# K and Q projections written transposed by the matmul, and plain loads in place of transposing DMAs, in a fused attention and FFN kernel

## The reference, cut to what matters

```python
xn = layernorm(x)                       # x: [4, 4096, 2048]
K = einsum('bse,ae->bsa', xn, Wk)       # a = 2048
Q = einsum('bse,ae->bsa', xn, Wq)
V = einsum('bse,ae->bsa', xn, Wv)
scores = einsum('bqa,bka->bqk', Q, K) / sqrt(2048)      # then the causal mask
attn = round(softmax(scores) @ V, 4 decimals)
ffn  = fake_quant(relu(fake_quant(xn) @ fake_quant(kernel) + fake_quant(bias)))
out  = x + attn + ffn
```

## Time and profile before

| | us |
|---|---|
| median of 2 runs | 5945.97 |
| the two runs | 5921.64 and 5970.3 |
| profiled execution | 5971.41 |
| its span, slowest core (core 4) | 5969.9 |
| spans of the other cores | 5839.6 to 5943.7 |

### The profile page before, as it was taken

How to read it: one execution, slowest core, us unless ns; L and a number is a source line. 1 busy time by engine, 2 the same in 40 slices (tenths; PEclk the granted TensorE clock), 3 DMA queues, 4 the chain that set the end, 5 groups by cost and what they waited for, 6 DMA issues and landing times.

```text
span 5969.9 us, 38440 instructions; the slowest of 8 cores (5839.6 to 5969.9 us)
## 1 busy us (share of the span) xinstructions
PE 3581.1 (60%) x9611; PEld 886.2 (15%) x9801; DVE 1084.3 (18%) x1473; ACT 655.8 (11%) x717; POOL 209.9 (4%) x87
## 2 busy tenths in 40 slices
PE   2877787878787466666206831336364537465776
PEld 0212212121212111111001210001010101111111
DVE  1111101010100322220495630111010101101001
ACT  1101101010100222221211210000000000000000
POOL 1000000000000000000050000000000000000000
PEclk9767867676769565667557965555555555555555
DMA  8011000101001411101321112322323233232422
GB/s 152 36 36 43 36 35 36 36 36 36 36 29 47 94 39 42 38 33 46 106 85 43 56 29 60 85 81 84 79 81 81 86 87 80 89 82 79 129 69 98
DMA packets 501827, 380.75 MB, mean 64 GB/s; under 512 B 429537, under 2 KB 429697, under 8 KB 487297
## 3 DMA queue, kind: packets, MB, share of 16 engines
q1 hardware_dynamic: 445362, 277.56, 16.7%
q10 hardware_dynamic: 49152, 75.51, 3.3%
q0 software_dynamic: 7120, 25.22, 2.6%
HBM read 243.94 MB, written 75.51 MB: 54 GB/s over the span
## 4 chain that ended last, share of the span: by engine, by line
PE 49%; DMA 16%; issue 11%; DVE 7%; SPq 6%; ACT 6%; another core or an unknown queue 4%; ACTq 0%; DVEq 0%; POOLq 0%
PE pspool L445 12%; DMA pool<-qS 10%; PE pspool L467 8%; PE pspool L987 8%; SPq L970 6%; PE pspool L625 5%; DMA pool<-vS 5%; PE pspool L849 4%; PE pspool L1043 4%; PE pspool L427 2%; PE pspool L1079 2%; ACT pool L334 2%; ACT pool L336 2%; PE pspool L364 1%
## 5 line engine op out<-in xcount | busy, mean ns | idle before, releaser
L987 PE MATMUL pspool<-pool 128*128 128x512 bf16 x1127 | 649.1, 585 | 858.9 <-DMA pool<-kS 667.1
L445 PE MATMUL pspool<-pool 128*128 128x512 bf16 x2001 | 871.5, 517 | 209.5 <-remote 40.7
L625 PE MATMUL pspool<-pool 128*128 128x512 bf16 x996 | 467.6, 545 | 133.0 <-ACT pool L632 42.9
L467 PE MATMUL pspool<-pool 128*128 128x512 bf16 x2005 | 494.4, 408 | 4.0 <-PE pspool L427 0.9
L849 PE MATMUL pspool<-pool 128*128 128x512 bf16 x1003 | 272.6, 392 | 223.8 <-remote 182.9
L1043 PE MATMUL pspool<-pool 128*128 128x512 bf16 x559 | 296.0, 599 | 135.5 <-DMA pool<-vS 81.4
L987 PEld LDWEIGHTS pspool<-pool 128*128 128x128 bf16 x1152 | 121.9, 106 | 1388.1 <-issue 1386.2
L1079 PE MATMUL pspool<-pool 128*128 128x512 bf16 x567 | 232.1, 554 | 111.1 <-DMA pool<-vS 107.3
L427 PE MATMUL pspool<-pool 128*128 128x128 bf16 x512 | 135.1, 268 | 248.7 <-DVE pool L351 191.4
L445 PEld LDWEIGHTS pspool<-pool 128*128 128x128 bf16 x2048 | 145.2, 102 | 903.1 <-issue 899.5
L467 PEld LDWEIGHTS pspool<-pool 128*128 128x128 bf16 x2048 | 210.4, 103 | 275.4 <-issue 71.7
(11 more groups left out here) (118 smaller groups left out, 1932.9 us busy)
## 6 DMA issues: line engine op xcount, KB each, us to landing
pool<-vS SPq DMA_DIRECT2D x288, 256.0 KB, 2.7
pool<-emb SPq DMA_DIRECT2D x32, 1024.0 KB, 5.9
pool<-x_own SPq DMA_DIRECT2D x32, 1024.0 KB, 5.5
pool<-fker SPq DMA_DIRECT2D x32, 1024.0 KB, 5.0
kS<-pool ACTq DMA_DIRECT2D x32, 512.0 KB, 2.6
vS<-pool ACTq DMA_DIRECT2D x32, 512.0 KB, 2.6
out<-pool ACTq DMA_DIRECT2D x16, 1024.0 KB, 4.0
pool<-kS SPq DMA_TRANSPOSE x576, 2.7
```

What stands on the lines that cost most here:

```text
L445: e.matmul(psB[:, fo:fo + fw], xnT[:, 512 * c + 128 * t:512 * c + 128 * t + 128], W1[:, E * c + fo:E * c + fo + fw], start=st, stop=sp),
L467: e.matmul(pv, xnT[:, 512 * c + 128 * t:512 * c + 128 * t + 128], W2[:, E * c + fo:E * c + fo + fw], start=st, stop=sp),
L625: e.matmul(psB[:, fo:fo + fw], xnT2[:, 512 * c + 128 * t:512 * c + 128 * t + 128], WQ[:, E * c + fo:E * c + fo + fw], start=st, stop=sp),
L987: st=(c == 0), sp=(c == NCH - 1): e.matmul(pa, qt[par][T][:, 128 * c:128 * c + 128], ktb[ks][:, 512 * c:512 * (c + 1)], start=st, stop=sp),
```

## The change

K and Q are computed already transposed. The weights become the stationary operand (128x128 blocks of `W1` or `WQ`) and the normalised strip `xnT` the moving one, so each result is 128 values of `a` by 512 rows. For each strip and each of the 16 blocks `ca` of `a`, 16 matmuls accumulate into one 512-column bank of `psB`, which is now split into four buffers `bK[0..3]` used in turn. ACT evicts each bank (128x512) into one of two small buffers and stores it. `kS` and `qS` are laid out as [16, 128, rows], so the attention stage loads its tiles with plain DMAs.

The number of matmuls, their size (128x512) and the number of weight loads stay as they were. The order around them changes: in stage 1 a strip is now V for all four tiles, then all of K, then the 16 transpose batches of the next strip in one piece; `pend` is gone. In stage 2 the layer norms of the next strip are recorded ahead of the strip's Q matmuls, and its 32 batches after them.

```diff
-    kS = nc.dram_tensor("kS", [S, E], BF16, kind="Internal").ap()
+    kS = nc.dram_tensor("kS", [NCH, 128, S], BF16, kind="Internal").ap()
-    qS = nc.dram_tensor("qS", [OWNT * 128, E], BF16, kind="Internal").ap()
+    qS = nc.dram_tensor("qS", [NCH, 128, OWNT * 128], BF16, kind="Internal").ap()
...
+        bK = [Buf(f"psK{r}") for r in range(4)]
...
-                for c in range(NCH):
-                    for fi, (fo, fw) in enumerate(_splits(E)):
-                        p.step("PE", lambda e, c=c, t=t, fo=fo, fw=fw,
-                               st=(c == 0), sp=(c == NCH - 1):
-                               e.matmul(psB[:, fo:fo + fw],
-                                        xnT[:, 512 * c + 128 * t:512 * c + 128 * t + 128],
-                                        W1[:, E * c + fo:E * c + fo + fw], start=st, stop=sp),
-                               reads=[b_xnTc[t], b_W1], writes=[bB[(2 * fo) // E]])
-                    if c % 4 == 3 and pend:
-                        fn = pend.pop(0)
-                        fn()
-                p.step("ACT", lambda e: e.activation(kev, psB[:, 0:E], AF.Copy),
-                       reads=[bB[0], bB[1]], writes=[b_kev])
...
+            xn_reads = [b_xnTc[0], b_xnTc[1], b_xnTc[2], b_xnTc[3], b_W1]
+            for ca in range(NCH):
+                r = ca % 4
+                pk = psB[:, 512 * r:512 * (r + 1)]
+                for ce in range(NCH):
+                    p.step("PE", lambda e, pk=pk, ca=ca, ce=ce,
+                           st=(ce == 0), sp=(ce == NCH - 1):
+                           e.matmul(pk, W1[:, E * ce + 128 * ca:E * ce + 128 * ca + 128],
+                                    xnT[:, 512 * ce:512 * ce + 512], start=st, stop=sp),
+                           reads=xn_reads, writes=[bK[r]])
+                ev = ca % 2
+                p.step("ACT", lambda e, pk=pk, ev=ev: e.activation(kste[ev], pk, AF.Copy),
+                       reads=[bK[r]], writes=[b_kste[ev]])
+                p.dma("ACT", "kev", lambda e, ca=ca, s=s, ev=ev: e.dma_start(
+                    out=kS[ca][:, 512 * s:512 * (s + 1)], in_=kste[ev]),
+                    reads=[b_kste[ev]], writes=[b_ktS])
+            if s + 1 < NSTRIP:
+                for t in range(4):
                     for j in range(NCH // 4):
-                        pend.append(lambda strip=s + 1, t=t, j=j: p1_tbatch(strip, t, j))
+                        p1_tbatch(s + 1, t, j)
...
         for so in range(NSO):
...
+            if so + 1 < NSO:
+                for t in range(4):
                     p2_ln(so + 1, t)
...
+                           e.matmul(pk, WQ[:, E * ce + 128 * ca:E * ce + 128 * ca + 128],
+                                    xnT2[:, 512 * ce:512 * ce + 512], start=st, stop=sp),
+                           reads=xn2_reads, writes=[bK[r]])
...
                         out=qt[par][T][:, 128 * c:128 * c + 128],
-                        in_=qS[128 * slot:128 * (slot + 1), 128 * c:128 * (c + 1)],
-                        transpose=True),
+                        in_=qS[c][:, 128 * slot:128 * (slot + 1)]),
                         reads=[b_qtS], writes=[b_qt[par][T]])
...
                         out=ktb[ks][:, 512 * c:512 * (c + 1)],
-                        in_=kS[512 * s:512 * (s + 1), 128 * c:128 * (c + 1)],
-                        transpose=True),
+                        in_=kS[c][:, 512 * s:512 * (s + 1)]),
                         reads=[b_ktS], writes=[b_ktb[ks]])
```

More of the change, by code:

```diff
@@ L493, in build_nc @@
         o_xnT2 = al.take(NCH * 512 // 2)
-        o_qev = al.take(E // 2)
+        o_qst = al.take(512)
         o_ci2 = al.take(E)
@@ L615, in build_nc @@
                 p2_nxbatch(0, t, j)
-        pend2 = []
         for so in range(NSO):
-            for t in range(4):
-                slot = 4 * so + t
-                for c in range(NCH):
-                    for fi, (fo, fw) in enumerate(_splits(E)):
-                        p.step("PE", lambda e, c=c, t=t, fo=fo, fw=fw,
-                               st=(c == 0), sp=(c == NCH - 1):
-                               e.matmul(psB[:, fo:fo + fw],
-                                        xnT2[:, 512 * c + 128 * t:512 * c + 128 * t + 128],
-                                        WQ[:, E * c + fo:E * c + fo + fw], start=st, stop=sp),
-                               reads=[b_xnT2c[t], b_WQ], writes=[bB[(2 * fo) // E]])
-                    if c % 2 == 1 and pend2:
-                        fn = pend2.pop(0)
-                        fn()
-                p.step("ACT", lambda e: e.activation(qev, psB[:, 0:E], AF.Copy, scale=RSQ),
-                       reads=[bB[0], bB[1]], writes=[b_qev])
-                p.dma("ACT", "qev", lambda e, slot=slot: e.dma_start(
-                    out=qS[128 * slot:128 * (slot + 1), :], in_=qev),
-                    reads=[b_qev], writes=[b_qtS])
-                if so + 1 < NSO:
-                    p2_ln(so + 1, t)
@@ new lines, in build_nc @@
+            if so + 1 < NSO:
+                for t in range(4):
+                    p2_ln(so + 1, t)
+            xn2_reads = [b_xnT2c[0], b_xnT2c[1], b_xnT2c[2], b_xnT2c[3], b_WQ]
+            for ca in range(NCH):
+                r = ca % 4
+                pk = psB[:, 512 * r:512 * (r + 1)]
+                for ce in range(NCH):
+                    p.step("PE", lambda e, pk=pk, ca=ca, ce=ce,
+                           st=(ce == 0), sp=(ce == NCH - 1):
+                           e.matmul(pk, WQ[:, E * ce + 128 * ca:E * ce + 128 * ca + 128],
+                                    xnT2[:, 512 * ce:512 * ce + 512], start=st, stop=sp),
+                           reads=xn2_reads, writes=[bK[r]])
+                ev = ca % 2
+                p.step("ACT", lambda e, pk=pk, ev=ev: e.activation(qste[ev], pk, AF.Copy, scale=RSQ),
+                       reads=[bK[r]], writes=[b_qste[ev]])
+                p.dma("ACT", "qev", lambda e, ca=ca, so=so, ev=ev: e.dma_start(
+                    out=qS[ca][:, 512 * so:512 * (so + 1)], in_=qste[ev]),
+                    reads=[b_qste[ev]], writes=[b_qtS])
```

26 lines of the change are left out of this document (9 added, 17 removed).

## The result

The changed kernel takes 0.9878 of the time of the kernel before (95% interval 0.9849 to 0.9907), 1.2% less, which is within the 2% that count here as no change. The medians are 5941.39 us (22 runs, 5861.74 to 6271.88) and 5958.78 us (21 runs); they lie closer together than the ratio says, because some runs of the changed kernel had a die at a lower clock than the other, and the ratio leaves those out. The profiled execution took 5867.34 us, its slowest core (core 7) 5865.8 us. The forecast of 6225 us and its range of 6100 to 6400 us were wrong, and so was the sign. What came is the rival "K keeps the fast clock throughout": 5879 us on the execution.

What follows compares the result with a forecast made beforehand. Projections bound by matmul spacing and granted clock, attention by K loads queued behind Q loads. 5971.4 + 299 (K and V) + 254 (Q) - 273 (attention) = 6251 us on the execution, scaled to a median of 6225; range 6100 to 6400.

Steps and rivals of the forecast that it cites:

- K keeps the fast clock throughout: Rival for stage 1: a K strip takes 129.5 instead of 176 us, execution 5879 us, median 5854; chance 0.13.
- Which clock?: K in stage 1: starts at 1.00, holds it some 18 us of each strip, then 0.50; a strip 176 us.
- V, mean of a strip: V in stage 1: first tile 15.0 us, others 13.6, three pauses of 2.2 us; 62.5 us a strip.
- transposes, a strip of stage 1: Stage 1: 64 transposes per strip, 0.415 us apart, 26.6 us, in seven strips.
- Q stays at 0.50 throughout: Q stage: the same chain at half clock after transposes, 16 groups of 11.45 us, 183 us a strip.
- Q, wait for ACT, three times: Q stage: layer norms ahead of evictions on ACT make PE wait after four groups, from 46 until 87.5 us.
- a plain load of Q in a group: Attention: 32 KB Q loads one after another take 2.0 us each, bounds 1.7 and 2.7; 64 us per group.
- wait before the first score: Start of attention: the wait before its first matmul shrinks from 173.3 to 141 us.
- wait for K loads, groups 1 to 6: Attention: first K block ready after 76.6 instead of 106.8 us, 30 us less per group, 181 us in all.
- wait for the first V load: Attention, four even groups: a wait of up to 15.0 us behind the K loads goes, 59 us together.
- rival with both at the fast clock: Rival: K and Q both run at the fast clock, execution 5705 us, median 5681 us; chance 0.04.
- rival in which plain loads bring nothing: Rival: issue and landing stay as for transposing loads, attention does not move; execution 6524 us, median 6496; chance 0.03.

Runs made afterwards that it cites:

- k_pause: The changed kernel with the first K group of each strip also waiting until DVE has evicted the last V tile; ratio to the kernel before 1.065.
- v_banks: The changed kernel with V tiles alternating between `psB` and `psA`/`psN`; second run's ratio to the kernel before 0.9746, the first gave none.
- before_plain: The kernel before with plain loads in attention in place of transposing ones, transposition left out so scores use wrongly arranged data; ratio to the kernel before 0.9581.
- k_first: The changed kernel with K ahead of V in every strip of stage 1, so K follows the transposes; ratio to the kernel before 1.0682.
- rotate: The changed kernel with K and Q going through four banks in turn, matmul by matmul, using eight banks; ratio to the kernel before 0.8223.

## Why the prediction was wrong, point by point

**The step that failed** is the one headed "Which clock?". It says: "Between 'falls at once' and 'holds all the strip' I choose, nearer to the score rows, that it holds for some 18 us of each strip", and so a K strip of 176 us. Measured: 129.5 us, 8 x 46.5 = 372 us less. With this one term put right the forecast on the execution is 5879 us; 5867 were measured. That the two lie so close is luck in part, for the other errors cancel: V +28, transposes of stage 1 -37, Q -24, attention +25 us, and -3 us between the stages. The prediction had noted that an idle 2.94 us stood ahead of the fall in the earlier trace rows, and that no row showed an uninterrupted chain losing 1.00, and then let the score chain speak for K all the same. The row showed two causes at once, a pause and a chain. k_pause parts them for K: with the pause the clock goes, without it the same chain holds it. The prediction gave 0.13 to the case that came, and its range ended above it.

The other steps, on the execution:

| step | forecast | measured |
|---|---|---|
| distance in the chain at 1.00 / 0.50 | 0.525 / 0.735 us | the same |
| V, mean of a strip | 62.5 us | 66.0 us |
| transposes, a strip of stage 1 | 26.6 us | 21.3 us |
| Q stays at 0.50 throughout | 183 us a strip plus a wait | yes |
| Q, wait for ACT, three times | 41.7 us | 43.0 us |
| Q, 128 transposes | 53 us | 43.7 us |
| a plain load of Q in a group | 2.0 us | 2.05 us |
| wait before the first score | 141 us | 129.5 us |
| wait for K loads, groups 1 to 6 | 48.3 us each | 54.6 us each |
| wait for the first V load | 59 us less | 50 us less (81.4 to 31.7) |

*Stage 1.* V's mean is what is left of 1712.9 us after eight K strips and seven times the transposes, (1712.9 - 1036 - 149)/8. So V took 8 x 3.5 = 28 us more than forecast: the first tile of a strip, which follows transposes, took 15.5 to 16.9 us instead of 15.0, some 10 us in eight strips, and 13.5 us went in the tiles that lost the clock for a moment behind their pauses (v_banks, above). The transposes took 7 x 5.3 = 37 us less, because without matmuls between them one batch runs into the next: within a batch they stand 0.41 us apart as before, but the first of a batch starts 0.13 us behind the last of the one before, 0.33 us on the mean; 2094 - 372 + 28 - 37 = 1713. The evictions of K were hidden, as forecast. So were the layer norms, whose waits at the transposes (191.4 us in 32 times before, above) are down to 62.1 us in the four ahead of the first strip; some 129 us of stage 1 went with them.

*Q.* Right in mechanism and nearly in size. The timeline shows the wait after the fourth group, and behind it the chain, three matmuls in 2.2 us:

```profile
2056.33 2.79 PE L627 MATMUL pspool<-pool 128*128 128x512 bf16 x4 [43.00 <-ACT pool L631]
2059.26 2.05 PE L627 MATMUL pspool<-pool 128*128 128x512 bf16 x3
```

Three times 9.3 us less for the transposes and three times 1.3 us more for the waits are the 24 us between 1017 and 992.6 us. The two stages side by side are the lesson of this case: the same chain ran at 1.00 in K and at 0.50 in Q, since K follows the dense V and Q follows transposes and a barrier. The rival with both at the fast clock did not come, and the Trainium skill's rule on it ("TensorE: Matmul & The Clock Gate", Loop structure matters more than you think: matmuls in a row with DMAs beside them stay warm) fits K but not Q: the last of its four strips has no wait for ACT and still stood at 0.50, 0.735 us apart, from its first matmul to its last.

*Attention.* 248 of 273 us. The first wait fell by 43.8 us instead of 33; per group some 23.5 us instead of 30 were gained, counted from SP's start on the group to PE's first score. The 32 Q loads took 66 instead of 64 us, the 16 issues of the first K block 9.2 instead of 7.5 us, and PE started 6.3 instead of 2.7 us behind the last of them, so these loads landed later than the forecast had them; the V wait brought 50 instead of 59 us. The 187 us less of `kS` and the 50 us less of `vS` are 237 of the 248. The rival in which plain loads bring nothing fell with before_plain. The Trainium skill ("Advanced Engine Details and Errata", X-Bar Transpose) has both kinds equally fast. For the landing of a K load that is nearly so, 2.7 us transposing and 2.9 us plain; a Q load landed in 1.8 instead of 2.3 us, and the queue's own time is another altogether. Of a group's gain, 13 us are the 32 Q loads one after another (78.9 to 65.8 us on the mean of six groups) and 15 us the issues of a K block (23.8 to 9.2 us), less 4.5 us of later landing.

## What to carry to other kernels

Before you price a matmul chain at one clock, look at what stands ahead of it: here dense work without a gap handed the fast clock on, transposes or a pause of 2.9 us did not, and the chain did not win it back; a reordering that moves a slow-starting loop behind a dense one can be worth more than the loop's own edits. When a row shows a fall with two candidates in front of it, the price of the other candidate belongs into the range. And where matmuls stand half a microsecond apart, first see which buffer they are said to write: four names instead of two took 11.6% off the old kernel, and the whole rewrite 1.2%.

## What the runs showed of the hardware that was not expected

- A chain of 128x512 matmuls 0.525 us apart held 1.00 for 129.5 us, eight times over; the same at 0.50 never rose, in 183 us of K in k_first, and in a Q stage of 992.6 us with transposes in between. 128x256 ones 0.417 us apart lost 1.00 after 6 us.
- 2.9 us without a weight load ahead of the chain cost 53.5 us a strip, some twenty times their own length. The two pauses of some 1.1 and 0.74 us ahead of a V tile brought the half clock too, in 8 of 24 tiles, but the dense matmuls won it back at a price of 1.69 us (15.23 less 13.54). The difference between a pause that costs 1.69 us and one that costs 53.5 us is what stands behind it.
- The clock column can be wrong before its first change. In k_first it says 1.00 for the first K strip, while the weight loads stand 0.73 us apart, a distance of the half clock; the distances decide:

```profile
130.00:160.00 30.00, 23.89 (x42) 4.30 (x42) 0.00 (x0) 1.19 (x2) 0.00 (x0) 1.00 0.03 9
```
```profile
130.25 0.10 PEld L447 LDWEIGHTS pspool<-pool 128*128 128x128 bf16 x1 [0.63 <-issue]
130.99 0.11 PEld L447 LDWEIGHTS pspool<-pool 128*128 128x128 bf16 x1 [0.63 <-issue]
```

- In rotate's first strip the granted clock stood at 0.81, neither of the two levels, and the dense matmuls 0.262 us apart, which is 0.213/0.81. In the next strip it was 1.00. Why was not tried.
- A plain 32 KB load landed in 1.8 us, next to 2.9 us for 128 KB, and overlapped ones kept SP for 0.48 us each (30.45/64).
